# The last expert of the last round: products by halves of the hidden units, weighted and added on VectorE, stored in two pieces

## The chip, the cores and the metric

One core of one Trainium2 chip runs the whole kernel. The metric is device time in microseconds (us). The kernel before takes 1095.29 us, the median of 3 runs (1094.91 to 1095.7). The profiled execution on which all the rows below rest took 1093.58 us, with a span of 1091.6 us from its first to its last instruction.

## The reference

A batch of 32 sequences of 256 tokens with 128 channels passes through a Mamba block and then a mixture of experts, each with a layer norm ahead of it and a residual around it. Only the mixture of experts is touched here:

```python
scores = x_flat @ gate_w.T
topk_scores, topk_idx = jax.lax.top_k(scores, TOPK)          # 2 of 8 experts
topk_probs = jax.nn.softmax(topk_scores, axis=-1)
cw = zeros((N, E)).at[arange(N)[:, None], topk_idx].add(topk_probs)
y = jnp.zeros_like(x_flat)
for e in range(E):                                           # E = 8, FF = 256
    h = jax.nn.silu(x_flat @ w1[e].T) @ w2[e].T
    y = y + cw[:, e:e + 1] * h
```

All eight experts are computed for every token, and the weight of an expert that a token did not choose is zero. Everything is float32.

## The kernel before

The 32 sequences are taken in 16 rounds of two sequences, 512 tokens each (T = 512). On the token side of the work a round is a tile of 128 partitions by TB = 4 blocks by C = 128 channels: block b holds the tokens b*128 to b*128+127, one on each partition. A round passes through many stages (load, norm, convolution, 16 state scans, output product, second norm, routing, experts, store), and the stages of up to seven rounds run side by side. Each engine has its own list of calls, written out by hand, in which the calls of different rounds alternate; there is no planner. The engines wait for each other with counting semaphores: `j.count(per, more)` is the value that a semaphore has after `more` steps of round j when a round adds `per` steps.

One expert e of a round takes five steps on four engines:

- TensorE, `hidden(j, e, f)` (line 1776): w1 for half f of the 256 inner units times the tokens, into one PSUM bank of 128 x 512. In float32 one call is 2 matmul instructions of 512 columns.
- ScalarE, `hidden` (line 889): silu of that bank into `hid[:, e % 2, f]` in SBUF, which counts up `hid_ready`.
- TensorE, `expert(j, e)` (line 1786): waits until both halves of `hid` are there, then multiplies: for each of the 4 token blocks b the two halves f, which accumulate in one quarter of a bank. 8 products are 16 matmul instructions of 128 columns. The last counts up `expert_done`.
- VectorE, `weight_expert(j, e)` (line 1310): one tensor_tensor of 128 x 512 multiplies the bank with the routing weight `cw` into `weighted[:, e % 2]`.
- GpSimd, `add_expert(j, e)` (line 574): one tensor_tensor of 128 x 512 adds `weighted` to `x1`, the residual stream of the round, in SBUF.

When all eight are added (`expert_added`), SyncE's queue stores the 256 KB of `x1` with one transfer (`store_out`, line 356), in runs of 512 bytes.

At the end of the program, after the scans of round 15 (the last), only this work is left. TensorE's list ends with expert(15, 5), hidden(15, 6, 1), hidden(15, 7, 0), expert(15, 6), hidden(15, 7, 1), expert(15, 7). ScalarE, VectorE and GpSimd have nothing after their part of expert 7 of round 15. SyncE issues the store of round 15, waits for `out_stored` of both parities (line 441), and then all engines meet in a last barrier (line 120). `MOVED` gives the PSUM bank of each step in the last rounds: expert(15, 6) uses bank 3, hidden(15, 7, 0) bank 5, hidden(15, 7, 1) bank 1 and expert(15, 7) bank 4. `y_ps` is a further pair of banks, in which the outputs of the state scans are summed; it is read out (`copy_y`, `yT_ready`) long before the last expert.

Of the kernel before, what the change touches and what calls it, by code (L numbers as in the profile page):

```python
# [5 lines left out]
ALU = mybir.AluOpType  # L6
# [5 lines left out]
P = 128  # L12
# [3 lines left out]
TB = T // P  # L16
# [9 lines left out]
E = 8  # L26
FH = 2
# [17 lines left out]
EXPERT = ("expert", (0, 1, 1, 0, 1, 1, 0, 1))  # L45
# [46 lines left out]
def mamba_moe(nc, x, W_in, conv_w, conv_b, W_x, W_dt, b_dt, A_log, D, W_out, gate_wT, w1T, w2T, out):  # L92
    rounds = x.shape[0] * x.shape[1] // T
    lead = Round(0, lead=True)
    r = [Round(k) for k in range(rounds)]
    x_v = x.rearrange("(i s) (b p) c -> i p (s b) c", s=SEQS, p=P)
    out_v = out.rearrange("(i s) (b p) c -> i p (s b) c", s=SEQS, p=P)
    c_dram = nc.dram_tensor("c_dram", (2, NS, T), F32).ap()

    def there(*js):  # L100
        return all(j.loop is not None or 0 <= j.at < rounds for j in js)

    def wait(eng, sem, value):

        if not isinstance(value, int) or value > 0:
            eng.wait_ge(sem, value)
# [13 lines left out]
    with ExitStack() as ctx:  # L120
        def sb(name, shape, dt=F32):
            return ctx.enter_context(nc.sbuf_tensor(name, shape, dt))

        def ps(name, shape):
            return ctx.enter_context(nc.psum_tensor(name, shape, F32))

        def sem(name):
            return ctx.enter_context(nc.semaphore(name))
# [13 lines left out]
        w2 = sb("w2", [P, FH, E, C])  # L142
# [37 lines left out]
        x1 = sb("x1", [P, 2, TB, C])  # L180
# [8 lines left out]
        cw = sb("cw", [P, 2, TB, E])  # L189
        hid = sb("hid", [P, 2, FH, T])  # L190
# [3 lines left out]
        y_ps = ps("y_ps", [P, H, TB, P])  # L194
# [27 lines left out]
        out_stored = [sem("out_stored0"), sem("out_stored1")]  # L222
# [35 lines left out]
        yT_ready = sem("yT_ready")  # L258
# [16 lines left out]
        hid_ready = sem("hid_ready")  # L275
        expert_done = sem("expert_done")
        expert_weighted = sem("expert_weighted")
        expert_added = sem("expert_added")

        LOADS = 4  # L280
        COPIES = 3 * H + 1
# [7 lines left out]
        def token_bank(k):  # L289

            return bank(k).rearrange("p (b c) -> p b c", b=TB)

        def bank(k):

            return work[:, k, :] if k < 2 else rows[:, (k - 2) // H, (k - 2) % H, :]

        def place(table, j, *at):

            name = table[0], rounds - j.at, *at
            if j.loop is None and name in MOVED:  # L300
                return MOVED[name]
            k = table[1]
            for a in at:
                k = k[a]
            return k

        def bcd_bank(j):
            return bank(LEAD_BCD if j.lead else BCD)

        def two_seqs(ap):  # L310
            return ap.rearrange("p (s t) -> p s t", s=SEQS)
# [16 lines left out]
        def _(sp):  # L328
# [22 lines left out]

            def store_out(j):
                if not there(j):
                    return
                sp.wait_ge(expert_added, j.count(E, E))
                sp.dma_start(out_v[j.number()], x1[:, j.odd]).then_inc(out_stored[j.odd], 16)
# [18 lines left out]
            def round_(i):  # L375
                three, four, five, seven = (i.later(-k) for k in (3, 4, 5, 7))
                load_again(five)
                load_c(four, 2)
                store_c(three)
                store_out(seven)  # L380
                load_c(four, 3)
                load_c(three, 0)
                load_c(three, 1)
                load_x(i)
# [49 lines left out]
            load_again(r[15])  # L434
            load_c(r[15], 3)
            store_out(r[12])
            store_out(r[13])
            store_out(r[14])
            store_out(r[15])
            for odd in range(2):  # L440
                sp.wait_ge(out_stored[odd], 16 * (rounds // 2))

        @block.gpsimd
        def _(pool):
# [122 lines left out]
                nc.gpsimd.tensor_tensor(cw[:, j.odd], picked[:, 0], picked[:, 1], ALU.add).then_inc(routing_step, 1)  # L567

            def add_expert(j, e):
                if not there(j):  # L570
                    return
                pool.wait_ge(expert_weighted, j.count(E, e + 1))
                wait(pool, expert_added, j.count(E, e))
                nc.gpsimd.tensor_tensor(x1[:, j.odd], x1[:, j.odd], weighted[:, e % 2],  # L574
                                        ALU.add).then_inc(expert_added, 1)

            def round_(i):
                two, three, four, five = (i.later(-k) for k in (2, 3, 4, 5))
                add_soft(two)
                times_u(two)  # L580
                add_expert(five, 4)
                outputs(three, 13)
                outputs(three, 14)
                add_expert(five, 5)
                gap(four)
                outputs(three, 15)
                outputs(two, 0)
                outputs(two, 1)
                outputs(two, 2)
                add_expert(five, 6)  # L590
                routing(four)
                add_expert(five, 7)
# [138 lines left out]
        def _(act):  # L731
# [52 lines left out]
            def copy_bcd(j):  # L784
                if not there(j) or j.led():
                    return
                act.wait_ge(bcd_projected, j.count(1, 1))
                wait(act, c_stored[1 - j.odd], j.later(-1).turn(16, 16))
                wait(act, c_used, j.count(NS, CGROUP - NS))
                nc.scalar.activation(bcd[C_ROW:ROWS, :], bcd_bank(j)[C_ROW:ROWS], ACT.Copy).then_inc(bcd_ready, 1)  # L790

            def high(j):
                if not there(j) or j.led():
                    return
                act.wait_ge(bcd_projected, j.count(1, 1))
                wait(act, b_ready, j.count(NS, -NS))
                wait(act, dt_projected, j.count(H, -H))
                nc.scalar.activation(parts[:, j.odd, :], bcd_bank(j)[0:3 * SPLIT], ACT.Copy).then_inc(high_ready, 1)

            def middle(j):  # L800
                if not there(j) or j.led():
                    return
                act.wait_ge(high_taken, j.count(1, 1))
                nc.scalar.activation(parts[0:2 * SPLIT, j.odd, :], bcd_bank(j)[0:2 * SPLIT],
                                     ACT.Copy).then_inc(middle_ready, 1)
# [417 lines left out]
        def _(dve):  # L1223
# [79 lines left out]
            def weight_expert(j, e):  # L1303
                if not there(j):
                    return
                dve.wait_ge(expert_done, j.count(E, e + 1))
                if e == 0:
                    dve.wait_ge(routing_step, j.count(ROUTING, ROUTING))
                wait(dve, expert_added, j.count(E, e - 1))
                nc.vector.tensor_tensor(weighted[:, e % 2], token_bank(place(EXPERT, j, e)),  # L1310
                                        cw[:, j.odd, :, e:e + 1].broadcast_to([P, TB, C]),
                                        ALU.mult).then_inc(expert_weighted, 1)

            def round_(i):
# [6 lines left out]
                inputs(three, 0)  # L1321
                scan(four, 15)
                weight_expert(six, 6)
                scan(three, 0)
                inputs(three, 1)
                scan(three, 1)
                inputs(three, 2)
                weight_expert(six, 7)
                scan(three, 2)
                inputs(three, 3)  # L1330
# [3 lines left out]
                scan(three, 4)  # L1334
                inputs(three, 5)
                weight_expert(five, 0)
                scan(three, 5)
                inputs(three, 6)
# [287 lines left out]
        def _(pe):  # L1626
            def free(*uses):

                for s, j, per, more in uses:
                    if there(j):  # L1630
                        pe.wait_ge(s, j.count(per, more))
                        return
# [146 lines left out]
            def expert(j, e, *uses):  # L1779
                if not there(j):  # L1780
                    return
                pe.wait_ge(hid_ready, j.count(E * FH, FH * (e + 1)))
                free(*uses)
                for b in range(TB):
                    for f in range(FH):
                        last = nc.tensor.matmul(token_bank(place(EXPERT, j, e))[:, b, :], hid[:, e % 2, f, b * P:(b + 1) * P],  # L1786
                                                w2[:, f, e, :], start=(f == 0), stop=(f == FH - 1))
                last.then_inc(expert_done, 1)
# [37 lines left out]
            def round_(i):  # L1826
# [16 lines left out]
                delta_rank(one, 1, use_hid(four, 4, 0), use_gate(one, 1))  # L1843
                sum_states(two, 7)
                expert(four, 3, use_hid(four, 4, 1))
                sum_states(two, 8)
                expert(four, 4, use_dt(one, 1), use_hid(four, 4, 0))
                row_b(two, 12)
                hidden(four, 5, 0, use_expert(four, 3))
# [491 lines left out]
```

## Time and profile before

| what | us |
|---|---|
| median of 3 runs | 1095.29 |
| lowest and highest run | 1094.91, 1095.7 |
| profiled execution | 1093.58 |
| its span | 1091.6 |
| PE busy | 1039.5 |
| DVE busy | 1016.8 |
| POOL busy | 961.8 |
| ACT busy | 908.1 |

PE is TensorE's matmuls, PEld its weight loads, DVE VectorE, ACT ScalarE, POOL GpSimd and SP SyncE. "SPq" is the queue of an engine that issues transfers or waits. The busy times are sums over the whole span; the change touches only the last 8 us of it, where these averages say little. In the views below a line of the timeline gives the start in us from the span's start, the length in us, the engine, the kernel's line, the instruction, what it writes and reads, and how many instructions are merged in it; the brackets give the idle time of the engine before it and what released it.

### The profile page before, as it was taken

The page shows a single profiled execution, that of the slowest core. Times are in us where ns is not written, and L with a number is a line of the kernel's source. Part 1 is how long each engine was busy: PE and PEld are TensorE (multiplying, and loading weights), DVE is VectorE, ACT ScalarE, POOL GpSimd, SP SyncE. Part 2 cuts the span into 40 slices and gives each one's busy share as a digit, 9 for nine tenths or more (in the row PEclk, how much of TensorE's full clock was granted, in tenths as well). Part 3 has the DMA queues.
Part 4 walks back from the last instruction along what each step waited for, and adds up shares of the span by engine and source line. Part 5 has one row for each costly group of instructions (what it writes and reads, how often), then busy time and mean ns, then how long its engine had stood idle before and what let it go on. Part 6 is the DMA issues. An engine that isn't in the chain of part 4 may idle for free.

```text
span 1091.6 us, 18705 instructions
## 1 busy us (share of the span) xinstructions
PE 1039.5 (95%) x6150; PEld 756.5 (69%) x6150; DVE 1016.8 (93%) x1054; ACT 908.1 (83%) x1379; POOL 961.8 (88%) x891
## 2 busy tenths in 40 slices
PE   7688779999999999999999999999999999989997
PEld 4446456677777767777777777767777776767775
DVE  5999999999999999999999999999999999999721
ACT  4987877989989998998989899899989989875533
POOL 4688986999999999999999999999999999799834
PEclk9798899999999999999999999999999999989999
DMA  5331212132040313104031311303130220320000
GB/s 201 138 127 57 78 60 79 59 117 69 6 167 14 127 59 122 63 30 153 2 126 58 126 58 64 120 0 130 54 136 39 88 87 0 137 87 11 11 10 11
DMA packets 37349, 84.12 MB, mean 77 GB/s; under 512 B 3305, under 2 KB 28193, under 8 KB 28961
## 3 DMA queue, kind: packets, MB, share of 16 engines
q1 hardware_dynamic: 36864, 83.06, 21.3%
q8 instruction: 25, 0.41, 0.2%
q14 instruction: 44, 0.35, 0.1%
q10 hardware_dynamic: 416, 0.30, 0.1%
HBM read 78.63 MB, written 4.72 MB: 76 GB/s over the span
## 4 chain that ended last, share of the span: by engine, by line
PE 82%; DVE 10%; issue 4%; ACT 3%; DMA 0%; POOL 0%; POOLq 0%; DVEq 0%; ACTq 0%
PE work L1786 19%; PE work L1776 18%; PE y_ps L1728 17%; PE work L1652 9%; DVE h L1241 6%; PE rows L1707 4%; PE work L1749 2%; PE work L1636 2%; PE work L1671 2%; PE rows L1786 2%; PE work L1662 2%; DVE rows L1231 2%; PE rows L1776 1%; PE work L1697 1%; PE y_ps L1717 1%
## 5 line engine op out<-in xcount | busy, mean ns | idle before, releaser
L534 POOL TENSOR_TENSOR h<-h,c_rows 128x1024 f32<-128x1024 f32 x256 | 600.4, 2368 | 52.2 <-DVE h L1241 52.1
L1241 DVE TENSOR_TENSOR_SCAN h<-dA,rows 128x1024 f32<-128x1024 f32 x256 | 579.4, 2277 | 1.1
L855 ACT ACTIVATE dA<-delta,a_neg 128x510 f32<-128x510 f32 x512 | 326.2, 709 | 8.0 <-DVE h L1241 4.6
L1231 DVE TENSOR_TENSOR rows<-du,rows 128x1024 f32<-128x1024 f32 x256 | 306.8, 1215 | 3.9 <-PE rows L1707 3.7
L1728 PEld LDWEIGHTS y_ps<-ident,h 128*128 128x128 f32 x2048 | 241.3, 144 | 61.5 <-issue 33.5
L1728 PE MATMUL y_ps<-ident,h 128*128 128x128 f32 x2048 | 270.0, 278 | 10.7 <-POOL h L534 10.7
L1786 PEld LDWEIGHTS work<-w,hid 128*128 128x128 f32 x1856 | 223.2, 193 | 35.1 <-ACT hid L889 18.9
L1776 PE MATMUL work<-x2T,w 128*128 128x512 f32 x474 | 238.5, 598 | 3.4 <-ACT u L773 2.8
L1786 PE MATMUL work<-w,hid 128*128 128x128 f32 x1856 | 229.1, 277 | 2.7 <-ACT hid L889 2.2
L889 ACT ACTIVATE hid<-work 128x512 f32<-128x512 f32 x237 | 139.4, 596 | 64.0 <-PE work L1776 62.2
L574 POOL TENSOR_TENSOR x<-x,weighted 128x512 f32<-128x512 f32 x128 | 163.6, 1278 | 21.6 <-DVE weighted L1310 21.1
L1776 PEld LDWEIGHTS work<-x2T,w 128*128 128x128 f32 x474 | 81.7, 190 | 57.3 <-issue 19.5
L1707 PE MATMUL rows<-parts,select 96*128 96x512 bf16 x256 | 100.3, 392 | 21.1 <-DVE h L1241 19.7
L1652 PE MATMUL work<-xnT,w_conv 128*128 128x512 f32 x256 | 116.3, 597 | 0.5 <-ACT xnT L765 0.5
L739 ACT ACT_TABLE_LOAD x74 | 94.9, 1283 | 1.3
L889 ACT ACT_TABLE_LOAD x56 | 71.8, 1283 | 20.5 <-PE work L1776 14.7
L1310 DVE TENSOR_TENSOR weighted<-work,cw 128x512 f32<-128x512 f32 x116 | 78.6, 677 | 8.6 <-PE work L1786 6.8
L1652 PEld LDWEIGHTS work<-xnT,w_conv 128*128 128x128 f32 x256 | 47.4, 191 | 49.0 <-issue 47.9
L1707 PEld LDWEIGHTS rows<-parts,select 96*128 96x128 bf16 x256 | 25.4, 100 | 56.7 <-DVE h L1241 28.5
L1310 DVE TENSOR_TENSOR weighted<-rows,cw 128x512 f32<-128x512 f32 x12 | 8.2, 691 | 32.3 <-PE rows L1786 20.5
L525 POOL TENSOR_TENSOR du<-delta,u 128x1024 f32<-128x1024 f32 x15 | 35.4, 2363 | 1.8 <-POOL delta L518 1.3
L518 POOL TENSOR_TENSOR delta<-du,soft 128x1024 f32<-128x1024 f32 x15 | 35.4, 2361 | 0.0
(141 smaller groups left out, 954.3 us busy)
## 6 DMA issues: line engine op xcount, KB each, us to landing
c_rows<-c_dram SPq DMA_DIRECT2D x64, 1024.0 KB, 4.8
x_in<-in_x SPq DMA_DIRECT2D x16, 256.0 KB, 2.9
x_again<-in_x SPq DMA_DIRECT2D x16, 256.0 KB, 3.4
out<-x SPq DMA_DIRECT2D x16, 256.0 KB, 2.6
w<-in_w1T SPq DMA_DIRECT2D x1, 1024.0 KB, 4.9
w<-in_w2T SPq DMA_DIRECT2D x1, 1024.0 KB, 7.1
h<-in_conv_w SPq DMA_DIRECT2D x1, 512.0 KB, 4.8
c_dram<-bcd SPq DMA_DIRECT2D x16, 32.0 KB, 1.6
```

The lines of the kernel that those rows point to most:

```text
L534: nc.gpsimd.tensor_tensor(at, at, c_rows[:, n, :].unsqueeze(1).broadcast_to([P, H, T]), ALU.mult).then_inc(c_used, 1)
L574: nc.gpsimd.tensor_tensor(x1[:, j.odd], x1[:, j.odd], weighted[:, e % 2], ALU.add).then_inc(expert_added, 1)
L739: nc.scalar.preload_act_table_set("natural_log_exp_and_others")
L855: last = nc.scalar.activation(two_seqs(dA[:, n % RING, half, :])[:, :, 1:], two_seqs(delta[:, half, :])[:, :, 1:], ACT.Exp, scale=a_neg[:, ...
L889: nc.scalar.activation(hid[:, e % 2, f, :], bank(place(HIDDEN, j, e, f)), ACT.Silu).then_inc(hid_ready, 1)
L1231: nc.vector.tensor_tensor(rows[:, n % 2], du[:, j.odd], rows[:, n % 2, H - 1, :].unsqueeze(1).broadcast_to([P, H, T]), ALU.mult).then_inc( ...
L1241: nc.vector.tensor_tensor_scan(h[:, n % RING].rearrange("p h t -> p (h t)"), dA[:, n % RING].rearrange("p h t -> p (h t)"), rows[:, n % 2] ...
L1652: last = nc.tensor.matmul(two_seqs(work[:, CONV[half], :]), w_conv[:, k, half * P:(half + 1) * P], xnT[:, :, k:k + SEQ], start=(k == 0), s ...
L1707: nc.tensor.matmul(rows[:, n % 2, H - 1, :], select[:, n, :], parts[:, j.odd, :], start=True, stop=True).then_inc(b_ready, 1)
L1728: last = nc.tensor.matmul(y_ps[:, half, b, :], h[:, n % RING, half, b * P:(b + 1) * P], ident[:, :], is_transpose=True, start=False, stop= ...
L1776: nc.tensor.matmul(bank(place(HIDDEN, j, e, f)), w1[:, e, f, :], x2T[:, j.odd, :], start=True, stop=True).then_inc(hid_projected, 1)
L1786: last = nc.tensor.matmul(token_bank(place(EXPERT, j, e))[:, b, :], hid[:, e % 2, f, b * P:(b + 1) * P], w2[:, f, e, :], start=(f == 0), s ...
```

## The change

For round 15 and expert 7 alone (`is_last`), and for nothing else:

- TensorE takes the products with the inner half f on the outside: first the four blocks with f = 0, as soon as `hid` half 0 is ready, then the four blocks with f = 1 after waiting for half 1. Blocks 0 and 1 go to the same bank as before (bank 4), blocks 2 and 3 to the first bank of `y_ps`. The last product of block 1 counts up `last_half_done`, that of block 3 `expert_done`.
- VectorE waits until GpSimd has added expert 6, and then, for each half of the tokens, computes `x1 = bank * cw + x1` with one scalar_tensor_tensor of 128 x 128 for each of the two blocks. It counts up `last_added` after each half.
- GpSimd's `add_expert(15, 7)` is gone.
- SyncE stores the two halves of the tokens with a transfer of 128 KB each, and waits at the end for one transfer more.

```diff
+        def is_last(j, e):
+
+            return j.loop is None and j.at == rounds - 1 and e == E - 1
+
+        def last_half_bank(half):
+
+            return token_bank(place(EXPERT, r[-1], E - 1)) if half == 0 else y_ps[:, 0]
+
...
             def store_out(j):
                 if not there(j):
+                    return
+                if is_last(j, E - 1):
+                    for half in range(2):
+                        some = slice(half * TB // 2, (half + 1) * TB // 2)
+                        sp.wait_ge(last_added, half + 1)
+                        sp.dma_start(out_v[j.number()][:, some, :], x1[:, j.odd, some, :]
+                                     ).then_inc(out_stored[j.odd], 16)
                     return
...
-                sp.wait_ge(out_stored[odd], 16 * (rounds // 2))
+                sp.wait_ge(out_stored[odd], 16 * (rounds // 2 + odd))
...
             def add_expert(j, e):
-                if not there(j):
+                if not there(j) or is_last(j, e):
                     return
...
             def weight_expert(j, e):
                 if not there(j):
                     return
+                if is_last(j, e):
+                    dve.wait_ge(expert_added, j.count(E, e))
+                    for half in range(2):
+                        if half == 0:
+                            dve.wait_ge(last_half_done, 1)
+                        else:
+                            dve.wait_ge(expert_done, j.count(E, E))
+                        for b in range(half * TB // 2, (half + 1) * TB // 2):
+                            at = x1[:, j.odd, b, :]
+                            last = nc.vector.scalar_tensor_tensor(at, last_half_bank(half)[:, b, :],
+                                                                  cw[:, j.odd, b, e:e + 1], at, ALU.mult, ALU.add)
+                        last.then_inc(last_added, 1)
+                    return
...
             def expert(j, e, *uses):
                 if not there(j):
                     return
-                pe.wait_ge(hid_ready, j.count(E * FH, FH * (e + 1)))
+                if not is_last(j, e):
+                    pe.wait_ge(hid_ready, j.count(E * FH, FH * (e + 1)))
                 free(*uses)
+                if is_last(j, e):
+                    pe.wait_ge(yT_ready, rounds)
+                    for f in range(FH):
+                        pe.wait_ge(hid_ready, j.count(E * FH, FH * e + f + 1))
+                        for b in range(TB):
+                            half, first = b // (TB // 2), b % (TB // 2) == 0
+                            last = nc.tensor.matmul(last_half_bank(half)[:, b, :], hid[:, e % 2, f, b * P:(b + 1) * P],
+                                                    w2[:, f, e, :], start=(first and f == 0),
+                                                    stop=(not first and f == FH - 1), skip_group_check=True)
+                            if f == FH - 1 and not first:
+                                last.then_inc((last_half_done, expert_done)[half], 1)
+                    return
```

## Rows read from the trace of the kernel before

**Rows 1.** The page, part 4: the chain that ended last, over the whole span.
```profile
PE 82%; DVE 10%; issue 4%; ACT 3%; DMA 0%; POOL 0%; POOLq 0%; DVEq 0%; ACTq 0%
```

**Rows 2.** Timeline of all engines in the tail, from 1081 us to the end.
```profile
1081.05 2.05 PE L1786 MATMUL rows<-w,hid 128*128 128x128 f32 x16
1081.26 0.60 ACT L889 ACTIVATE hid<-rows 128x512 f32<-128x512 f32 x1 [0.26 <-PE rows L1776]
...
1082.94 1.02 PE L1776 MATMUL work<-x2T,w 128*128 128x512 f32 x2
1083.14 0.69 DVE L1310 TENSOR_TENSOR weighted<-rows,cw 128x512 f32<-128x512 f32 x1 [2.97 <-PE rows L1786]
1083.91 1.27 POOL L574 TENSOR_TENSOR x<-x,weighted 128x512 f32<-128x512 f32 x1 [2.39 <-DVE weighted L1310]
1084.06 0.60 ACT L889 ACTIVATE hid<-work 128x512 f32<-128x512 f32 x1 [2.20 <-PE work L1776]
...
1084.71 2.05 PE L1786 MATMUL rows<-w,hid 128*128 128x128 f32 x16 [0.75 <-ACT hid L889]
1086.80 0.69 DVE L1310 TENSOR_TENSOR weighted<-rows,cw 128x512 f32<-128x512 f32 x1 [2.97 <-PE rows L1786]
1087.57 1.26 POOL L574 TENSOR_TENSOR x<-x,weighted 128x512 f32<-128x512 f32 x1 [2.39 <-DVE weighted L1310]
...
1088.86 0.37 SPq L356 DMA_DIRECT2D out<-x  x1
```

**Rows 3.** Waits of SyncE's queue from 1085 us on: total us, times, longest.
```profile
SPq L356 <- POOL x L574: 28.3, 1, 28.3
SPq L441 <- DMA out<-x: 1.9, 1, 1.9
```

**Rows 4.** Instructions of line 441, the wait for the last store.
```profile
L441 SPq EVENT_SEMAPHORE  x1: 17/17/17, 1091.2 to 1091.2; - x1
```

**Rows 5.** Timeline at 1073 us: a hidden product and an expert behind it without a gap.
```profile
1072.97 1.02 PE L1776 MATMUL rows<-x2T,w 128*128 128x512 f32 x2
...
1073.84 1.95 PE L1786 MATMUL rows<-w,hid 128*128 128x128 f32 x16
```

**Rows 6.** Line 1786 from 1076 us on: count, ns minimum/median/maximum of one.
```profile
L1786 PE MATMUL rows<-w,hid x48: 275/275/377, 1077.4 to 1086.5; 128*128 128x128 f32 x48
```

**Rows 7.** Timeline of VectorE at 8 us and at 13 us: short instructions.
```profile
8.12 0.16 DVE L1395 SCALAR_TENSOR_TENSOR shift<-mean_variance,rstd 128x4 f32<-128x4 f32 x1 [0.94 <-POOL rstd L469]
8.32 0.60 DVE L1399 TENSOR_SCALAR xn<-x_in,rstd,shift 128x128 f32<-128x128 f32 x2
...
13.34 0.87 DVE L1249 BATCH_NORM_STATS2 stats<-x_in 128x6 f32<-128x128 f32 x4
```

**Rows 8.** VectorE's groups by form: count, busy us, mean ns of one.
```profile
L1399 DVE TENSOR_SCALAR xn<-x_in,rstd,shift 128x128 f32<-128x128 f32 x2 | 0.6, 342 | 0.0
```

**Rows 9.** Timeline of SyncE's queue at 22 us: four transfers issued one behind the other.
```profile
22.11 1.96 SPq L372 DMA_DIRECT2D c_rows<-c_dram  x4
```

**Rows 10.** The page, part 6: DMA issues, count, KB each, median us to landing.
```profile
out<-x SPq DMA_DIRECT2D x16, 256.0 KB, 2.6
...
c_dram<-bcd SPq DMA_DIRECT2D x16, 32.0 KB, 1.6
```

**Rows 11.** DMA view from 1085 us: the last store alone, issue to landing.
```profile
DMA packets 528, 0.26 MB, mean 37 GB/s; under 512 B 16, under 2 KB 528, under 8 KB 528
...
out<-x SPq DMA_DIRECT2D x1, 256.0 KB, 2.3
```

**Rows 12.** DMA view of 1089.6 to 1091.3 us: GB/s in 40 slices of 0.0425 us.
```profile
GB/s 0 0 0 24 120 241 301 277 337 265 313 265 313 265 313 265 313 265 313 265 313 265 313 265 278 181 85 12 0 0 0 0 0 0 0 0 0 0 0 0
```

**Rows 13.** The DMA view over the whole span: a transfer of 128 KB, with its landing.
```profile
w_out<-in_W_out SPq DMA_DIRECT2D x1, 128.0 KB, 2.0
```

**Rows 14.** Lines 350 and 356: us from issue to landing, minimum/median/maximum of all transfers.
```profile
DMA to landing us min/median/max: 3.0/3.4/11.7
...
DMA to landing us min/median/max: 2.3/2.6/2.7
```

More of the change, by code:

```diff
@@ L278, in mamba_moe @@
         expert_added = sem("expert_added")
+        last_half_done = sem("last_half_done")
+        last_added = sem("last_added")
         LOADS = 4
```

## The prediction

> **What bounds the kernel now.** I read the page's chain of waits first, then the timeline of the tail on all engines, then the waits of SyncE's queue and the DMA view of the last store. The chain is PE's for 82% of the span [rows 1], but the change leaves everything before the last expert alone, so what matters is what stands between TensorE's last work and the end. The timeline of the tail [rows 2] is a plain relay in which each engine waits for the one before it:
>
> - 1082.94: the second hidden product of expert 7 starts; ScalarE's silu of it runs 1084.06 to 1084.66; PE has idled meanwhile (0.75 us in the row) although the other half of `hid` has been ready since 1081.86.
> - 1084.71 to 1086.76: 16 matmuls of expert 7.
> - 1086.80 to 1087.49: weighting on VectorE. 1087.57 to 1088.83: addition on GpSimd.
> - 1088.86: the store is issued. It lands 2.3 us later [rows 11], at 1091.16, which fits the release of SyncE's last wait at 1091.2 [rows 3, 4]. From there the barrier takes 0.44 us to the end of the span at 1091.6, and 1.98 us lie outside the span in the profiled execution (1093.58 less 1091.6). Neither part changes.
>
> So every microsecond taken out of this relay is one microsecond of the kernel; nothing runs beside it that could become the end instead. The end is hidden by no other work.
>
> **The change part by part.**
>
> *TensorE.* A matmul of 128 columns starts every (1.95 - 0.275)/15 = 0.112 us in a run without a gap [rows 5, 6]. The four products with f = 0 are 8 instructions, 0.89 us. They can follow the hidden product as the expert does in rows 5, where it starts 0.87 us behind the start of the hidden product: 1082.94 + 0.87 = 1083.81, done issuing at 1084.70. The silu of the other half is seen by PE at 1084.71, so the 8 instructions fit the idle time almost exactly. The waits added to PE (half 0 of `hid`, `yT_ready`) are long met, and nothing is queued behind them but these products. The f = 1 products begin at 1084.71 as before, but are 8 instead of 16: the end moves from 1086.76 to 1086.76 - 0.89 = 1085.87, and the first half of the tokens is ready 4 instructions earlier, at 1085.42. PE gains 0.89 us; the bounds are 0 (if the early products bought nothing) and 0.89.
>
> *VectorE and GpSimd.* The path loses 0.69 us of weighting, 0.08 us of hand-over and 1.26 us of addition [rows 2]. It gains four scalar_tensor_tensor of 128 x 128 from PSUM with a scalar from memory, a form the trace lacks. The nearest row is tensor_scalar of 128 x 128 with two such scalars: 0.342 us for one, 0.60 us for two, so a second starts 0.26 us after the first [rows 7, 8]. The cheap side is bn_stats on 128 x 128, four in 0.87 us, so one each 0.20 us [rows 7], and a scalar_tensor_tensor on 4 columns at 0.16 us. The dear side within reason is 0.342 us each without overlap; beyond that, 0.69 us each, the full row of 512 columns [rows 2]. I take 0.26 us from start to start and 0.34 us for the last, the row with the same size and kind of operand. VectorE's own new wait is for GpSimd's addition of expert 6; that ends at 1083.91 + 1.27 = 1085.18, ahead of 1085.42, with 0.24 us to spare. Behind it stands only this work. With 0.04 us from PE to VectorE as at 1086.80: start 1085.46, first half done 1085.46 + 0.60 = 1086.06, third instruction at 1085.98 (its data came at 1085.91), second half done 1085.98 + 0.60 = 1086.58.
>
> *SyncE.* The hand-over to its queue took 0.03 us (1088.83 to 1088.86). The first issue is at 1086.09. Four transfers issued in a row took 1.96 us, 0.49 us each [rows 9], so the second could go at 1086.58; its data is there at 1086.61. Thus the extra issue hides behind the second half's arithmetic. The last issue moves from 1088.86 to 1086.61: 2.25 us. Bounds of this term: 2.0 with 0.342 us without overlap (1085.46 + 4 x 0.342 = 1086.83, issue 1086.86), and 2.4 with the bn_stats rate (then SyncE's spacing decides: first issue 1085.97, second 1086.46).
>
> *The store.* 256 KB landed in 2.3 us. Its packets moved in the fourth to the 28th slice of the close view [rows 12], that is from 1089.73 to 1090.79, 1.06 us in all. Half the bytes at that rate are about 0.5 us less, landing 1.8 us after the issue. Other sizes: 128 KB in 2.0 us [rows 13], though that one is a load with other transfers near it; 32 KB in 1.6 us, 256 KB in 2.6 us in the median [rows 10]. I take 1.95 us, a saving of 0.35 us; the bounds are 0 (2.3 us whatever the size) and 0.7 (1.6 us). The first piece's packets would run from about 1086.96 (0.87 us behind its issue, as before) to 1087.5, and the second's begin at 1086.61 + 0.87 = 1087.48: they hardly meet.
>
> Sum: 2.25 + 0.35 = 2.60 us. By the profiled execution the time becomes 1093.58 - 2.60 = 1090.98; that execution lay 1.7 us under the median of the runs, so against the median it is 1095.29 - 2.6 = 1092.7 us.
>
> [...] The store of 128 KB is not seen in the trace, and the Trainium skill, DMA: Bandwidth & Descriptors (Anatomy of one DMA), prices a transfer at about 2.0 us fixed plus bytes/436e3; that is 2.60 us for 256 KB, where the trace has 2.3 to 2.7 us [rows 14], and an estimated 2.30 us for half of it. By it the store would save 0.30 us and the sum be 2.55. [...]
>
> **The rivals.**
>
> *A. The blocks are dear on VectorE.* For it: no row has this form with a source in PSUM. Against it: a scalar_tensor_tensor of 4 columns took 0.16 us, and the ends of all forms of 128 columns lie under 0.35 us. At 0.69 us each: 1085.46 + 2.76 = 1088.22, issue 1088.25, a gain of 0.6 + 0.35 = 0.95 us; at 0.5 us each 1.7 us. Time about 1094.
>
> *B. The early products buy nothing* (PE does not begin them in the gap, or ScalarE's silu slips by as much). For it: the gap is filled to the last 0.01 us. Against it: rows 5 show an expert following a hidden product without a gap. The second half is then ready at 1086.76, its two blocks end at 1087.40 and the issue is at 1087.43: gain 1.43 + 0.35 = 1.8 us, time 1093.5.
>
> *C. The two stores run one after the other*, the second moving only when the first has landed: 1086.09 + 1.95 + 1.95 = 1089.99 against 1091.16, gain 1.2 us, time 1094.1. Against it: the packets of one store fill only 1.06 of its 2.3 us, the rest is latency that two transfers can share.
>
> *D. The second store is held up behind the first so far that the kernel becomes slower.* Transfers issued close behind others can land very late: up to 11.7 us against a median of 3.4 us for `x_again` [rows 14]. It decides from a landing of 1091.16 - 1086.61 = 4.55 us on; at the 11.7 us of the worst row the end moves by 7.15 us, to 1102.4 us. Against it: nothing but 128 KB stands ahead of it, and a store alone has never taken over 2.7 us.
>
> **How the numbers follow.** A measurement of this kernel can tell about 0.2%, 2.2 us, from no change, so the forecast lies just beyond that line. The forecast's case has 0.74: its bounds are a gain of 2.0 + 0 to 2.4 + 0.5 us, and I give 0.60 to the part over 2.2 us and 0.14 to the part below. A has 0.07, B 0.06, C 0.08, all within 0.2%; D has 0.05 and is slower. That makes faster 0.60, same 0.35, slower 0.05. The runs spread by 0.4 us to each side. The range reaches from 1095.29 - 3.0 - 0.5 = 1091.8 to a gain of 1.2 with 0.2 for the spread, 1094.3, which takes in B and C and leaves out A's far end and D.
>
> **What would show it.** Right: the first eight matmuls of expert 7 directly behind the hidden product, the others from about 1084.7 for 1.15 us; the four VectorE instructions within about 1.1 us, beginning before PE is done; two store issues 0.5 us apart, the last near 1086.6; a landing about 2 us later. Wrong: VectorE released by GpSimd and not by PE; more than 0.35 us from start to start of its blocks; a second landing over 2.3 us after its issue; or a start of the tail that has itself moved, since nothing before 1082.9 is supposed to.

## The result, and the profile after

| | before | after |
|---|---|---|
| median of 11 runs each, us | 1094.91 | 1092.1 |
| profiled execution, us | 1093.58 | 1092.1 |
| its span, us | 1091.6 | 1090.0 |
| start of the last hidden product, us | 1082.94 | 1083.95 |
| from there to the end of the span, us | 8.66 | 6.05 |

The ratio of the two kernels is 0.9975, with a 95% interval of 0.9965 to 0.9985: 2.7 us faster, between 1.6 and 3.8 us. The forecast was 1092.7 us and a gain of 2.6 us. One of the eleven executions before took 2172.23 us, about twice the others, and the ratio leaves it out; without it the median before is 1094.65 us. In a second series the same kernel came out at 0.998 (0.9971 to 0.9989), 2.2 us (1.2 to 3.2 us). The change is clear of no change in both, but a timing alone can't say on which side of the forecast's line of 2.2 us it lies.

The last two lines of the table say it more finely. The execution after reached the last hidden product 1.01 us later than the one before, on identical work, and yet ended 1.6 us earlier. Everything the change touches lies behind that product, so I measure every kernel by its tail: from the start of the last hidden product (`hidden(15, 7, 1)`) to the end of the span. The tail went from 8.66 to 6.05 us, a gain of 2.61 us. The end of a span is printed to 0.1 us, so a tail is good to 0.05 us and a difference of two tails to 0.1 us; differences of starts within one timeline are good to about 0.01 us, and where less than 0.1 us matters I go by the start of the last store's issue.

The timeline of the tail after, PE, ACT, POOL, DVE and SyncE's queue, answers to that of before [rows 2]. L1821 is the new product, L1332 the new VectorE instruction, L369 the new stores, and L1806 and L591 are the lines 1776 and 574 of before:

```profile
1083.95 1.02 PE L1806 MATMUL work<-x2T,w 128*128 128x512 f32 x2
1084.15 0.69 DVE L1340 TENSOR_TENSOR weighted<-rows,cw 128x512 f32<-128x512 f32 x1 [2.97 <-PE rows L1829]
...
1084.81 0.61 PE L1821 MATMUL rows<-w,hid 128*128 128x128 f32 x4
...
1084.92 1.26 POOL L591 TENSOR_TENSOR x<-x,weighted 128x512 f32<-128x512 f32 x1 [2.39 <-DVE weighted L1340]
1085.07 0.60 ACT L906 ACTIVATE hid<-work 128x512 f32<-128x512 f32 x1 [2.20 <-PE work L1806]
...
1085.26 0.61 PE L1821 MATMUL y_ps<-w,hid 128*128 128x128 f32 x4
...
1085.72 0.71 PE L1821 MATMUL rows<-w,hid 128*128 128x128 f32 x4
...
1086.27 0.61 PE L1821 MATMUL y_ps<-w,hid 128*128 128x128 f32 x4
1086.56 0.61 DVE L1332 SCALAR_TENSOR_TENSOR x<-rows,cw,x 128x128 f32<-128x128 f32 x2 [1.71 <-PE rows L1821]
1087.08 0.60 DVE L1332 SCALAR_TENSOR_TENSOR x<-y_ps,cw,x 128x128 f32<-128x128 f32 x2
1087.19 0.89 SPq L369 DMA_DIRECT2D out<-x  x2
```

The first eight products now run under ScalarE's silu. VectorE begins 0.32 us before TensorE has finished and goes from the first half to the second without a pause. The line of the two stores ends at 1088.08; a store's issue takes 0.37 us, so the second is issued at 1087.71. The DMA view of the same stretch has its landing, and the waits of SyncE's queue what was left to wait for, 1.5 us against 1.9 [rows 3]:

```profile
out<-x SPq DMA_DIRECT2D x2, 128.0 KB, 1.8
```

```profile
SPq L369 <- DVE x L1332: 25.6, 1, 25.6
SPq L458 <- DMA out<-x: 1.5, 1, 1.5
```

Laid beside the prediction, all in us from the start of the last hidden product:

| step | before | predicted | after |
|---|---|---|---|
| products of half 1 begin | 1.77 | 1.77 | 1.77 |
| TensorE done | 3.82 | 2.93 | 2.93 |
| VectorE begins | 3.86 | 2.52 | 2.61 |
| `x1` complete | 5.89 | 3.64 | 3.73 |
| last store issued | 5.92 | 3.67 | 3.76 |
| landing, from the issue | 2.3 | 1.95 | 1.8 |
| end of the span | 8.66 | 6.06 | 6.05 |

### The profile page after: what moved, and what is told of

The parts are those of the page before. It is cut to its first block, busy times and chain, and to the rows that moved or that the text cites. A ratio compares the mean times of both kernels' runs of the same rounds, so it can differ in the third digit from the quotient of the medians.

```text
span 1090.0 us, 18707 instructions
## 1 busy us (share of the span) xinstructions
PE 1040.8 (95%) x6150; PEld 758.0 (70%) x6150; DVE 1017.5 (93%) x1057; ACT 907.1 (83%) x1379; POOL 959.6 (88%) x890
## 4 chain that ended last, share of the span: by engine, by line
PE 83%; DVE 9%; issue 4%; ACT 3%; DMA 0%; POOL 0%; DVEq 0%; ACTq 0%; POOLq 0%
PE work L1829 19%; PE work L1806 18%; PE y_ps L1758 18%; PE work L1682 8%; DVE h L1258 6%; PE rows L1737 4%; PE work L1779 3%; PE work L1666 2%; PE work L1701 2%; PE rows L1829 2%; PE work L1692 2%; PE rows L1806 1%; DVE rows L1248 1%; PE y_ps L1747 1%; PE work L1727 1%
## 5 line engine op out<-in xcount | busy, mean ns | idle before, releaser
L1806 PE MATMUL work<-x2T,w 128*128 128x512 f32 x474 | 240.2, 602 | 2.9 <-ACT u L790 2.3
L591 POOL TENSOR_TENSOR x<-x,weighted 128x512 f32<-128x512 f32 x127 | 161.9, 1274 | 19.6 <-DVE weighted L1340 19.2
L1806 PEld LDWEIGHTS work<-x2T,w 128*128 128x128 f32 x474 | 82.2, 191 | 56.8 <-issue 19.0
L790 ACT ACTIVATE u<-work,conv_bias 128x512 f32<-128x512 f32 x32 | 22.0, 687 | 15.5 <-PE work L1682 15.3
```

Of the source, the lines that this page charges most:

```text
L1806: nc.tensor.matmul(bank(place(HIDDEN, j, e, f)), w1[:, e, f, :], x2T[:, j.odd, :], start=True, stop=True).then_inc(hid_projected, 1)
```

## The experiments

Theory: the tail is a chain, and each of the three parts (TensorE's order, VectorE's fused blocks, two stores) shortens it by what the prediction worked out. The rivals are those of the prediction: A, the blocks are dear; B, the early products buy nothing; C and D, the second store waits or is held up. Each kernel is read by its tail. One store, the old block order, TensorE's order alone, VectorE's part alone, the order of the waits, four stores and the serial stores were each executed once, with a profile; the other four have 5 to 11 executions.

**One store.**

```diff
-                    for half in range(2):
-                        sp.wait_ge(last_added, half + 1)
-                        sp.dma_start(... one half ...)
+                    sp.wait_ge(last_added, 2)
+                    sp.dma_start(out_v[j.number()], x1[:, j.odd]).then_inc(out_stored[j.odd], 16)
```

> The changed kernel with one store of 256 KB after both halves. Measured: the tail, from the start of the last hidden product to the end of the span (8.66 us before, 6.05 us after). Theory (the second piece saves only the packet time of the first half; its issue hides behind VectorE): last issue at 3.76 us as in the changed kernel, landing 2.3 us later in place of 1.8, tail 6.5 us. Rival (the landing does not depend on the bytes, splitting buys nothing): tail 6.05 us.

The timeline of this kernel, and then the DMA view of its store:

```profile
1083.65 1.02 PE L1803 MATMUL work<-x2T,w 128*128 128x512 f32 x2
...
1087.41 0.37 SPq L367 DMA_DIRECT2D out<-x  x1
```

```profile
out<-x SPq DMA_DIRECT2D x1, 256.0 KB, 2.3
```

The tail is 1090.2 - 1083.65 = 6.55 us. The issue stands at 3.76 us, just where the second store's issue is in the changed kernel, so the extra issue costs nothing, and splitting is worth 0.5 us: the 2.3 against 1.8 us of landing.

**Blocks of tokens in the old order.**

```diff
-                    for f in range(FH):
-                        pe.wait_ge(hid_ready, j.count(E * FH, FH * e + f + 1))
-                        for b in range(TB):
+                    pe.wait_ge(hid_ready, j.count(E * FH, FH * (e + 1)))
+                    for b in range(TB):
+                        for f in range(FH):
```

> The changed kernel, but TensorE waits for both halves of the hidden units and takes the blocks of tokens one after the other, as before; banks, VectorE and stores stay as changed. Theory (the early products take 0.89 us off the path, and the halves of the tokens are then 0.9 us apart): the second half's products end 3.82 us after the last hidden product starts, last issue at 4.5 us, tail 6.75 us. Rival B (the early products buy nothing): tail 6.05 us.

The timeline of this kernel:

```profile
1083.01 1.02 PE L1806 MATMUL work<-x2T,w 128*128 128x512 f32 x2
...
1084.87 1.13 PE L1821 MATMUL rows<-w,hid 128*128 128x128 f32 x8 [0.84 <-ACT hid L906]
1085.83 1.06 PE L1821 MATMUL y_ps<-w,hid 128*128 128x128 f32 x8
1086.12 0.61 DVE L1332 SCALAR_TENSOR_TENSOR x<-rows,cw,x 128x128 f32<-128x128 f32 x2 [2.22 <-PE rows L1821]
1086.76 1.18 SPq L369 DMA_DIRECT2D out<-x  x2
1086.93 0.61 DVE L1332 SCALAR_TENSOR_TENSOR x<-y_ps,cw,x 128x128 f32<-128x128 f32 x2 [0.20 <-PE y_ps L1821]
```

Tail 1089.8 - 1083.01 = 6.79 us: 0.74 us more than the changed kernel, and 0.80 us more at the last issue (1087.57 - 1083.01 = 4.56 against 3.76). TensorE ends at 3.88 in place of 2.93. Most of that is the 0.89 us of its eight late instructions; the rest is that its products begin at 1.86 in place of 1.77, after an idle time of 0.84 us against 0.75 [rows 2]. VectorE gives some of it back: here it waits 0.20 us for the second half, while in the changed kernel the second half's products, done at 2.93, wait for VectorE until 3.13.

**TensorE's order alone**, with the old weighting, addition and store, all four blocks in one bank.

```diff
+                    for f in range(FH):
+                        pe.wait_ge(hid_ready, j.count(E * FH, FH * e + f + 1))
+                        for b in range(TB):
+                            ... start=(b == 0 and f == 0), stop=(b == TB - 1 and f == FH - 1)
+                    last.then_inc(expert_done, 1)
```

> Only TensorE's part of the change: products by halves of the hidden units, into one bank; weighting, GpSimd's addition and the single store as before. Theory: PE ends 0.89 us earlier and the rest of the relay (0.69, 1.26 us and the store's 2.3 us) is unchanged, tail 7.77 us. Rival B: tail 8.66 us.

The timeline of this kernel:

```profile
1085.01 1.02 PE L1786 MATMUL work<-x2T,w 128*128 128x512 f32 x2
...
1085.87 2.07 PE L1800 MATMUL rows<-w,hid 128*128 128x128 f32 x16
...
1087.97 0.69 DVE L1320 TENSOR_TENSOR weighted<-rows,cw 128x512 f32<-128x512 f32 x1 [2.08 <-PE rows L1800]
1088.74 1.26 POOL L584 TENSOR_TENSOR x<-x,weighted 128x512 f32<-128x512 f32 x1 [1.49 <-DVE weighted L1320]
...
1090.03 0.37 SPq L366 DMA_DIRECT2D out<-x  x1
```

Tail 1092.8 - 1085.01 = 7.79 us, a gain of 0.87 us. B falls: the sixteen matmul instructions run without a gap from 0.86 us on. Note the whole time of this execution, 1094.76 us, over the 1093.62 us of the kernel before on the same chip. By the time alone this part would look harmful.

**VectorE's part alone.**

```diff
+                    dve.wait_ge(expert_added, j.count(E, e))
+                    dve.wait_ge(expert_done, j.count(E, E))
+                    for b in range(TB):
+                        last = nc.vector.scalar_tensor_tensor(at, token_bank(...)[:, b, :], cw[...], at, ...)
```

> Only VectorE's part of the change: four scalar_tensor_tensor after all products, GpSimd's last addition gone; TensorE's order and the single store as before. Theory (0.26 us from one block to the next): 1.12 us in place of 2.07 us with hand-overs, issue at 5.0 us, tail 7.75 us. Rival A (blocks dear): at 0.34 us each without overlap 8.0 us, at 0.5 us each 8.65 us.

The timeline of this kernel:

```profile
1083.43 1.02 PE L1799 MATMUL work<-x2T,w 128*128 128x512 f32 x2
...
1085.20 2.05 PE L1810 MATMUL rows<-w,hid 128*128 128x128 f32 x16 [0.75 <-ACT hid L903]
1087.38 1.12 DVE L1325 SCALAR_TENSOR_TENSOR x<-rows,cw,x 128x128 f32<-128x128 f32 x4 [3.05 <-PE rows L1810]
1088.53 0.37 SPq L367 DMA_DIRECT2D out<-x  x1
```

Tail 1091.3 - 1083.43 = 7.87 us, a gain of 0.79 us where I expected 0.91. The four blocks take 1.12 us, exactly 3 x 0.26 + 0.34, so A falls. The miss is the start: 1087.38 is 0.13 us behind TensorE's end (1085.20 + 2.05 = 1087.25), where the old weighting is 0.04 us behind it [rows 2].

**The order of VectorE's two waits**, to find those 0.09 us, which the changed kernel has too (products done at 1086.43, VectorE at 1086.56).

```diff
-                    dve.wait_ge(expert_added, j.count(E, e))
...
                             dve.wait_ge(last_half_done, 1)
+                            dve.wait_ge(expert_added, j.count(E, e))
```

> The changed kernel with VectorE's two waits ahead of the first half in the other order: first for TensorE's products, then for GpSimd's addition of expert 6, which has long been met by then. Theory (VectorE began 0.13 us behind TensorE in the changed kernel and 0.04 us behind it in the kernel before; the wait that is met last costs 0.09 us more where another one stands ahead of it in the list): first block 0.04 us behind TensorE, tail 5.96 us. Rival (a scalar_tensor_tensor from PSUM simply starts 0.09 us later than a tensor_tensor): tail 6.05 us.

The timeline of this kernel:

```profile
1082.24 1.02 PE L1806 MATMUL work<-x2T,w 128*128 128x512 f32 x2
...
1084.01 0.71 PE L1821 MATMUL rows<-w,hid 128*128 128x128 f32 x4
...
1084.76 0.61 DVE L1332 SCALAR_TENSOR_TENSOR x<-rows,cw,x 128x128 f32<-128x128 f32 x2 [1.63 <-PE rows L1821]
1085.29 0.60 DVE L1332 SCALAR_TENSOR_TENSOR x<-y_ps,cw,x 128x128 f32<-128x128 f32 x2
```

VectorE is 0.04 us behind the products (1084.01 + 0.71 = 1084.72), the last issue stands at 3.68 us in place of 3.76, and the tail is 1088.2 - 1082.24 = 5.96 us. It is the order of the waits and not the instruction. The second half in the old block order says the same: it has a single wait ahead of the same instruction, and starts 0.04 us behind its products (1085.83 + 1.06 = 1086.89, start 1086.93).

**A bank for each block.**

```diff
-            return token_bank(place(EXPERT, r[-1], E - 1)) if half == 0 else y_ps[:, 0]
+            return (token_bank(place(EXPERT, r[-1], E - 1)), y_ps[:, 0], y_ps[:, 1], token_bank(0))[half]
...
+                    for b in range(TB):
+                        dve.wait_ge(last_half_done, b + 1)
+                        nc.vector.scalar_tensor_tensor(... last_half_bank(b) ...).then_inc(last_added, 1)
```

> The changed kernel with each block of 128 tokens in a PSUM bank of its own, so that VectorE can take block 0 while TensorE writes block 1; VectorE is released block by block, the two stores are as changed. Theory (the blocks are ready about 0.22 us apart, VectorE needs 0.26 us for each and now starts when GpSimd has added expert 6): last issue at 3.5 us in place of 3.76, tail 5.8 us. Rival (VectorE pays more for blocks that each wait): tail 6.05 us or more.

The timeline of this kernel:

```profile
1083.69 1.02 PE L1801 MATMUL work<-x2T,w 128*128 128x512 f32 x2
...
1084.66 1.28 POOL L591 TENSOR_TENSOR x<-x,weighted 128x512 f32<-128x512 f32 x1 [2.39 <-DVE weighted L1335]
...
1085.46 0.49 PE L1815 MATMUL rows<-w,hid 128*128 128x128 f32 x2
...
1086.07 0.35 DVE L1328 SCALAR_TENSOR_TENSOR x<-rows,cw,x 128x128 f32<-128x128 f32 x1 [1.49 <-PE rows L1815]
...
1086.34 0.60 DVE L1328 SCALAR_TENSOR_TENSOR x<-y_ps,cw,x 128x128 f32<-128x128 f32 x2
...
1086.86 0.34 DVE L1328 SCALAR_TENSOR_TENSOR x<-work,cw,x 128x128 f32<-128x128 f32 x1
```

Tail 1089.5 - 1083.69 = 5.81 us, the last issue at 3.54 us against 3.76, as expected, and a ratio to the kernel before of 0.9974 (0.9965 to 0.9983), which does not tell it from the changed kernel. VectorE's blocks still start 0.26 to 0.27 us apart, so the separate waits cost nothing here. Whether blocks released one by one need banks of their own was not tried. GpSimd's addition of expert 6 ends at 1085.94 and the products of the first block at 1085.95, so this kernel alone can't say which of the two VectorE waits for.

**Expert 6 on VectorE as well**, so that GpSimd's addition is out of the way.

```diff
+                if is_last(j, e + 1):
+                    dve.wait_ge(expert_added, j.count(E, e))
+                    for b in range(TB):
+                        last = nc.vector.scalar_tensor_tensor(...)
+                    last.then_inc(sixth_added, 1)
```

> As four banks, with the calls in the old order, and expert 6 too added on VectorE in place of GpSimd. Theory (in four banks it is GpSimd's addition of expert 6 that releases VectorE): TensorE's last block becomes the bound, last issue at 3.43 us, tail 5.67 us from the start of the last hidden product. Rival (VectorE is its own bound): tail 5.8 us as with four banks.

The timeline of this kernel:

```profile
1084.86 1.02 PE L1810 MATMUL work<-x2T,w 128*128 128x512 f32 x2
...
1086.63 0.49 PE L1824 MATMUL rows<-w,hid 128*128 128x128 f32 x2
...
1087.23 0.35 DVE L1329 SCALAR_TENSOR_TENSOR x<-rows,cw,x 128x128 f32<-128x128 f32 x1 [1.04 <-PE rows L1824]
```

Tail 1090.7 - 1084.86 = 5.84 us (ratio 0.9969, 0.9959 to 0.998): the rival was right. VectorE began expert 7 at 2.37 us, against 2.38 us with GpSimd's addition in the way. What releases it is the first block's products, and from there its own four blocks are the bound. The row of the kernel with four banks had named PE as the releaser, and my theory went against it.

**The last hidden product ahead of expert 6**, and both experts on VectorE.

```diff
-            expert(r[15], 6, use_expert(r[15], 4))
             hidden(r[15], 7, 1, use_hid(r[15], 5, 1))
+            expert(r[15], 6, use_expert(r[15], 4))
```

> As four banks, and besides: the last hidden product goes ahead of expert 6, the products of expert 7 are taken block by block, and expert 6 too is added on VectorE by four scalar_tensor_tensor. Measured from the start of hidden(15, 7, 0), from which the tail is 11.46 us before and 8.85 us after. Theory: TensorE has no gap left, VectorE's eight blocks are the bound, tail 8.45 us. Rival (VectorE starts expert 7 only when expert 6 is done and so loses what the order gains): tail 8.6 us or more.

Here the tail starts with `hidden(15, 7, 0)`. It begins at 1080.15 in the timeline of this kernel, at 1081.15 in that of the changed one:

```profile
1080.15 1.02 PE L1810 MATMUL rows<-x2T,w 128*128 128x512 f32 x2
...
1081.01 1.02 PE L1810 MATMUL work<-x2T,w 128*128 128x512 f32 x2
...
1081.87 1.95 PE L1830 MATMUL rows<-w,hid 128*128 128x128 f32 x16
...
1083.65 0.61 PE L1824 MATMUL rows<-w,hid 128*128 128x128 f32 x4
1083.86 1.12 DVE L1337 SCALAR_TENSOR_TENSOR x<-rows,cw,x 128x128 f32<-128x128 f32 x4 [3.67 <-PE rows L1830]
...
1085.02 0.35 DVE L1329 SCALAR_TENSOR_TENSOR x<-rows,cw,x 128x128 f32<-128x128 f32 x1
```

The tail is 1088.5 - 1080.15 = 8.35 us, against 8.85 after and 11.46 before. That is 0.1 us less than expected. TensorE has no gap left, and VectorE pauses only 0.04 us between the two experts. With expert 6 on VectorE but the hidden product in its old place (the experiment before this one) the same tail is 1090.7 - 1082.06 = 8.64 us, so it is TensorE's new order that gains. The median is 1090.3 us, the ratio 0.9964 (0.9951 to 0.9977): the shortest tail of this study, though its interval overlaps those of the others.

**Four stores.**

```diff
+                    for b in range(TB):
+                        sp.wait_ge(last_added, b + 1)
+                        sp.dma_start(out_v[j.number()][:, b, :], x1[:, j.odd, b, :]).then_inc(...)
```

> As four banks, but the residual stream is stored in four pieces of 64 KB, each when its block is added. Tail from the start of the last hidden product to the end of the span. Theory (SyncE's queue needs about 0.5 us for each issue, more than VectorE's 0.26 us for a block): issues at 2.75, 3.25, 3.75 and 4.2 us, landing 1.65 us after the last, tail 6.3 us, later than with two pieces (5.81 us). Rival (only the last piece's bytes count): issue at 3.5 us, tail 5.6 us.

The timeline of this kernel, whose last line is the fourth store alone, and then from the DMA view the GB/s in 40 slices of 0.1 us from 1085 us on:

```profile
1082.16 1.02 PE L1800 MATMUL work<-x2T,w 128*128 128x512 f32 x2
...
1084.92 1.77 SPq L368 DMA_DIRECT2D out<-x  x4
1085.33 0.34 DVE L1327 SCALAR_TENSOR_TENSOR x<-work,cw,x 128x128 f32<-128x128 f32 x1
...
1086.26 0.43 SPq L368 DMA_DIRECT2D out<-x  x1
```

```profile
GB/s 0 0 0 0 0 0 0 41 251 261 103 0 82 292 236 46 0 159 287 190 21 26 205 287 133 5 0 0 0 0 0 0 0 0 0 0 0 0 0 0
```

Tail 1088.4 - 1082.16 = 6.24 us, about 0.4 us worse than two pieces: the last issue stands at 4.10 us against 3.54, and the landing takes 1.6 us against 1.8. The data is complete at 1085.67, but SyncE's queue issues the last piece only at 1086.26. The holes in the GB/s row show that the DMA engines starve between the pieces; the issue is the bound, not the bytes.

**Stores one after the other**, rival C made true.

```diff
                         sp.wait_ge(last_added, half + 1)
+                        sp.wait_ge(out_stored[j.odd], 16 * (rounds // 2 - 1 + half))
```

> The changed kernel with the second store issued only when the first has landed, which is rival C of the prediction made true. Theory (in the changed kernel the two stores share their latency): first issue at 3.24 us, landing at 5.04, second issue at 5.1 and landing at 6.9, tail 7.35 us. Rival (the stores already ran one after the other): tail 6.05 us.

The timeline of this kernel, whose last line is the second store alone:

```profile
1083.89 1.02 PE L1807 MATMUL work<-x2T,w 128*128 128x512 f32 x2
...
1087.14 2.25 SPq L370 DMA_DIRECT2D out<-x  x2
...
1089.01 0.37 SPq L370 DMA_DIRECT2D out<-x  x1
```

Tail 1091.3 - 1083.89 = 7.41 us. The changed kernel's 6.05 us can only be had with the two stores overlapping, so C falls. D falls by the landings themselves: in all eight profiles with two stores each piece landed 1.8 to 1.9 us after its issue.

**The changed kernel again**, beside the timed versions.

> The changed kernel once more, on the chip of the next three, to compare them with it. Theory: tail (from the start of the last hidden product to the end of the span) 6.05 us, the whole 2.6 us below the kernel before. Rival (part of the measured difference is where the executions happened to fall in their spread): tail the same, the difference in the medians off by up to 1 us.

Tail 1088.4 - 1082.32 = 6.08 us, the same to the rounding. The ratio of 0.998 is 0.0005 above that of the first series, well inside both intervals. The tail repeats where the total does not: the two profiled executions of this kernel took 1092.1 and 1090.46 us.

## Why the prediction was right

- *TensorE.* Right in both terms: 1.77 and 2.93 us as worked out, and 0.87 us for the order alone.
- *VectorE.* The rate taken from the tensor_scalar row was right to 0.01 us, and the halves do follow without a pause. The start was 0.09 us late. The step that was off is "With 0.04 us from PE to VectorE as at 1086.80": that hand-over was taken from a row in which the wait met last (for TensorE) stands ahead of the other one; in the change it stands behind it.
- *GpSimd.* Its addition of expert 6 ended at 2.23 us against VectorE's start at 2.61, and did not matter.
- *SyncE.* The second issue hid behind the second half's arithmetic as said, 0.52 us behind the first. At the last issue the gain was 5.92 - 3.76 = 2.16 us in place of 2.25.
- *The store.* Half the bytes saved 0.5 us, not 0.35. The term was sized between the packet arithmetic (0.5) and a load of 128 KB; the packet arithmetic alone would have been right. The bounds of this term were 0 and 0.7, but the upper bound of the sum took 0.5 for it without a reason; by the term it should have been 0.7.

At the last issue the gain was overstated by 0.09 us, and in the landing it was understated by about 0.15 us. That the two nearly cancelled is luck, and so is the agreement of 2.60 and 2.61, which is closer than the 0.1 us to which a difference of tails is known; the mechanism is what was foreseen. Luck, too, lies in the median of 1092.1 us against the forecast 1092.7: single executions of the changed kernel lie between 1090.09 and 1093.65 us. The question on which the forecast gave 0.60, whether the gain is beyond 2.2 us, is left open by both series of timings, and is answered only by the tail.

The estimate of 0.30 us for the halved store, worked out from the price that the Trainium skill, DMA: Bandwidth & Descriptors (Anatomy of one DMA), gives for a transfer issued by GpSimd, was too low here, where SyncE issued: 256, 128 and 64 KB landed in 2.3, 1.8 and 1.6 us. The Trainium skill, VectorE: DVE Perf Modes (The TRN2 errata), gives a VectorE instruction with its source in PSUM 120 cycles plus one for each element at 0.96 GHz, an estimated 0.26 us for a block of 128; the trace agrees from start to start (0.26 us), while a block by itself took 0.34 us.

The parts alone give 0.87 (order), 0.79 (VectorE) and about 0.5 us (two stores, taken away from the whole): 2.16 us. The remaining 0.45 us come from weighting by halves, which lets VectorE work beside TensorE. That does not need TensorE's new order: with the blocks in the old order the gain was 8.66 - 6.79 = 1.87 us, 0.58 more than VectorE's 0.79 and the stores' 0.5. The order then adds 0.74 in place of the 0.87 it gives alone.

The spread of the total lies outside the change. Over the profiles of the kernel before, of the changed one (two) and of the nine experiments that leave the order of the calls alone, the last hidden product starts anywhere from 1082.16 to 1085.01 us, on work that none of them alters. The kept traces place it: the first store of a round is issued at 234.91 us in the kernel before, at 235.66 and 233.68 in the two profiles of the changed kernel, and anywhere from 233.68 to 236.81 over the twelve profiles, while from that store to the last hidden product all twelve take 847.96 to 848.64 us. So nearly all of the spread is made before that store, where no kernel differs from the others. What makes it there was not tried and stays open. In the second series the changed kernel's executions even fall into two groups, five at 1090.38 to 1090.87 and six at 1092.59 to 1093.65 us, so a median says little there.

## What to carry to other kernels

The last relay of a kernel is worth cutting by pieces, because nothing hides it: start what already has its inputs, fuse the last two steps on the engine that can read the products, and let the store begin before the work is complete. Two pieces were enough here, where the issues of stores stood 0.39 to 0.48 us apart and the arithmetic of a quarter took 0.26 us; four pieces ended about 0.4 us later. For changes of a few microseconds in a kernel whose total spreads by 3 us, measure from a fixed instruction shortly ahead of the change to the end of the span, where the two profiles of the changed kernel agreed to within the rounding.

## What the runs showed of the hardware

- Of two waits on VectorE, the order matters: 0.12 to 0.13 us from the products to the start where the one that is met last stands second (the changed kernel, VectorE's part alone), 0.04 us where it stands first (the kernel before, the wait order experiment), which there moved the last issue by 0.08 us. On TensorE the old block order, with its wait for `hid` behind two others, started 0.09 us later than the kernel before, which has it first; that was not tried by itself, and what causes either is not known.
- A scalar_tensor_tensor of 128 x 128 in float32, from PSUM with a scalar from memory, takes 0.34 us by itself, and four in a row take 1.12 us (VectorE's part alone).
- The last store of the kernel before divides into 0.87 us from issue to first packet, the packets (256 KB in 1.06 us), and about 0.4 us from the last packet to landing. With four pieces, where the queue itself was the bound, the issues stood at 1084.92, 1085.31, 1085.79 and 1086.26, 0.39 to 0.48 us apart.
